# Attention's RMS of parts 4 and 5 taken with tokens on partitions

## What is computed

```python
out = (x - mean) * rsqrt(var + 1e-5) * weight + bias          # layer norm
x = (out + tanh(cond @ lin_w.T + lin_b)) * weight + bias
x = x + a_alpha * attention(a_gamma * rms(x) + a_beta)        # 16 heads of 16
x = x + f_alpha * (silu(h @ gate_w.T) * (h @ hidden_w.T) @ out_w.T + out_b),  h = f_gamma * rms(x) + f_beta
```

## Time and profile before

| | |
|---|---|
| median of 3 runs | 960.4 us (960.19 to 960.7) |
| the profiled execution's own time | 959.94 us |
| its span | 958.1 us |
| granted TensorE clock | 0.999 |
| busy: PE, DVE, ACT, POOL | 919.5, 740.5, 634.9, 501.0 us |

### The profile page before, as it was taken

One profiled execution on the slowest core, in us unless ns is written; L12 is line 12 of the kernel. 1 busy time (PEld: TensorE's weight loads), 2 busy tenths in 40 slices (PEclk: granted clock), 3 DMA queues, 4 the chain that ended last, 5 costly groups with the idle time before them and its releaser, 6 DMA issues.

```text
span 958.1 us, 28583 instructions
## 1 busy us (share of the span) xinstructions
PE 919.5 (96%) x11064; PEld 883.9 (92%) x11064; DVE 740.5 (77%) x1433; ACT 634.9 (66%) x1837; POOL 501.0 (52%) x479
## 2 busy tenths in 40 slices
PE   5667999999999999999999999999999999999997
PEld 4557999999999999999999999999999999998997
DVE  5977788788778778877877887887788787667654
ACT  3656766767776776777677677767667766766432
POOL 4686455465655555555455555545555555453320
PEclk9999999999999999999999999999999999999999
DMA  6200011120020212002121210202110110100000
GB/s 224 75 2 29 13 24 56 25 51 22 10 57 24 57 24 51 13 18 57 23 57 24 49 12 20 58 24 56 25 36 23 24 36 18 18 13 13 13 12 24
DMA packets 40631, 33.77 MB, mean 35 GB/s; under 512 B 10800, under 2 KB 39984, under 8 KB 40496
## 3 DMA queue, kind: packets, MB, share of 16 engines
q1 hardware_dynamic: 40496, 31.93, 13.3%
HBM read 23.37 MB, written 8.55 MB: 33 GB/s over the span
## 4 chain that ended last, share of the span: by engine, by line
PE 89%; DVE 5%; issue 3%; POOL 2%; ACT 1%; DMA 0%; SPq 0%; DVEq 0%; ACTq 0%; POOLq 0%
PE psum L361 18%; PE psum L363 18%; PE psum L362 18%; PE psum L587 6%; PE psum L589 6%; PE psum L588 6%; PE psum L521 5%; PE psum L495 4%; PE psum L537 4%; PE psum L396 2%; PE psum L415 1%; DVE least L743 1%; PE psum L408 1%; POOL probs L1270 0%; DVE row_sum L759 0%
## 5 line engine op out<-in xcount | busy, mean ns | idle before, releaser
L361 PE MATMUL psum<-xf_hi,ffn_hi 128*128 128x256 f32 x1024 | 291.3, 284 | 2.1 <-ACT probsT L1055 1.6
L362 PE MATMUL psum<-xf_lo,ffn_hi 128*128 128x256 f32 x1024 | 288.1, 281 | 0.0
L363 PE MATMUL psum<-xf_hi,ffn_lo 128*128 128x256 f32 x1024 | 287.8, 281 | 0.0
L1047 ACT ACTIVATE probs<-psum,least 128x64 f32<-128x64 f32 x928 | 204.5, 354 | 38.5 <-DVE least L743 37.7
L1270 POOL TENSOR_TENSOR probs<-probs,inv_sum 128x512 f32<-128x512 f32 x128 | 133.9, 1047 | 154.1 <-DVE inv_sum L764 154.0
L361 PEld LDWEIGHTS psum<-xf_hi,ffn_hi 128*128 128x128 f32 x1024 | 192.7, 188 | 3.2 <-issue 2.7
L362 PEld LDWEIGHTS psum<-xf_lo,ffn_hi 128*128 128x128 f32 x1024 | 192.8, 188 | 0.0
L363 PEld LDWEIGHTS psum<-xf_hi,ffn_lo 128*128 128x128 f32 x1024 | 192.8, 188 | 0.0
L1076 ACT ACTIVATE prod_hi<-late 128x512 fp32r<-128x512 f32 x128 | 83.3, 651 | 127.6 <-DVE late L827 127.5
L587 PE MATMUL psum<-prod_hi,ffn_hi 128*128 128x256 f32 x512 | 144.1, 281 | 0.9 <-DVE prod_lo L833 0.9
L589 PE MATMUL psum<-prod_hi,ffn_lo 128*128 128x256 f32 x512 | 144.1, 282 | 0.0
(11 more groups left out here) (116 smaller groups left out, 2154.4 us busy)
## 6 DMA issues: line engine op xcount, KB each, us to landing
out_t_dram<-x_res SPq DMA_DIRECT2D x31, 256.0 KB, 3.0
xin<-x_dram SPq DMA_DIRECT2D x15, 512.0 KB, 6.7
shift_tok<-shift_rows SPq DMA_DIRECT2D x104, 64.0 KB, 3.1
inv_row<-inv_rows SPq DMA_DIRECT2D x26, 128.0 KB, 4.8
w_raw<-attn_w_dram SPq DMA_DIRECT2D x1, 1024.0 KB, 6.7
x_res<-gate_w_dram SPq DMA_DIRECT2D x1, 1024.0 KB, 9.4
late<-hidden_w_dram SPq DMA_DIRECT2D x1, 1024.0 KB, 11.3
w_raw<-out_w_dram SPq DMA_DIRECT2D x1, 1024.0 KB, 6.4
```

The costliest lines, as they stand in the source:

```text
L361: pe.matmul(out, stat_hi, mov_hi, start=first, stop=False)
L362: pe.matmul(out, stat_hi, mov_lo, start=False, stop=False)
L363: return pe.matmul(out, stat_lo, mov_hi, start=False, stop=last)
L1047: op = act.activation(probs[g % 4][:, h * SEQ:(h + 1) * SEQ], scores[g % 2][:, h // 2, h % 2], ACT.Exp, bias=least[g % 2][:, h:h + 1], sca ...
```

## The change

`ROW_FROM` goes from 6 to 4, so that parts 4 and 5 (block 2) are handled in the second way. A new function `root_due(s)` names the part whose inverses are taken and sent in slot `s`: for parts 4 and 5 in the last slot (`j == 3`) of the group ahead, slots 7 and 11, and for the later parts in the first slot of their group, as before. VectorE's residual, ScalarE's squares and GpSimd's sums of these parts, and GpSimd's `normalise_tokens` of block 2, go. `attention_out(1)` no longer waits for `scaled_a`.

```diff
--- before.py
+++ after.py
@@ -64,7 +64,7 @@
 SPLIT_ORDER = [c for chunks in SPLITS.values() for c in chunks]
 OUT_W_AT = -3
 QUAD = 32
-ROW_FROM = 6
+ROW_FROM = 4
 
 
 def conditioned_block(nc, x, cond_t, mod_w, feat_vecs, attn_w, gate_w, hidden_w, out_w, identity, head_mask, out_t):
@@ -221,6 +221,10 @@
             if not ROW_FROM // 2 <= b < NBLK or k not in (0, 1, 2, 4):
                 return None
             return 4 * b + min(k, 3)
+
+        def root_due(s):
+            m = (s + 1) // PSEQ + 2 if s < FFN_AT else s // PSEQ + 2
+            return m if row_part(m) and s % PSEQ == (3 if s < FFN_AT else 0) and s != FFN_AT else None
 
         def tile_no(i):
             return i - 2 * ROW_FROM
@@ -337,8 +341,8 @@
                     sp.dma_start(shift_rows, rows[:, D:2 * D]).then_inc(table_sent, 16)
                 if tile_at(s + 1) is not None:
                     load_shift(tile_at(s + 1))
-                if s % PSEQ == 0 and row_part(s // PSEQ + 2):
-                    send_inverses(s // PSEQ + 2)
+                if root_due(s) is not None:
+                    send_inverses(root_due(s))
                 if (s + 4) % (2 * PSEQ) == 0 and (s + 4) // (2 * PSEQ) + 2 < NBLK:
                     b = (s + 4) // (2 * PSEQ) + 2
                     sp.wait_ge(x_turned, 2 * (b - 1))
@@ -463,7 +467,8 @@
             def attention_out(m):
                 pe.wait_ge(att_lo_made, m + 1)
                 if early_out(m):
-                    pe.wait_ge(scaled_a, m + 4)
+                    if turns_a(m + 1):
+                        pe.wait_ge(scaled_a, m + 4)
                     if m >= 1:
                         pe.wait_ge(scaled_f, m)
                 else:
@@ -892,13 +897,13 @@
                     mean_squares_out(grp)
                 if is_step(f - 1):
                     product_lo(f - 1)
-                if j == 0 and row_part(grp + 2):
-                    token_squares_out(grp + 2)
+                if root_due(s) is not None:
+                    token_squares_out(root_due(s))
                 if j == 1 and tile_at(s) is not None and tile_at(s) % TILES == 3:
                     shift_tokens(tile_at(s))
                 if s == 0:
                     scale_a(1)
-                if j == 0 and PSEQ <= s <= FFN_AT:
+                if j == 0 and PSEQ <= s <= FFN_AT and not row_part(grp + 2):
                     make_residual(grp + 2)
                 if s % 2 == 0:
                     for g in (s, s + 1):
@@ -1130,10 +1135,10 @@
                 if s == 0:
                     split_hi_a(1)
                 if wide(s) and j == 0 and s > 0:
-                    square_a(grp + 2)
+                    if turns_a(grp):
+                        square_a(grp + 2)
                     keys_out(grp + 1)
                 if s == FFN_AT:
-                    square_a(grp + 2)
                     keys_out(grp + 1)
                     square_f(grp - 2)
                 if s % 2 == 0 and is_seq(s):
@@ -1289,7 +1294,8 @@
                     apply_beta_a(1)
                     split_lo_a(1)
                 if j == 0 and 0 <= s < FFN_AT:
-                    sum_squares_a(grp + 2)
+                    if turns_a(grp):
+                        sum_squares_a(grp + 2)
                     if is_part(grp - 2):
                         sum_squares_f(grp - 2)
                 if j == 2 and 0 <= s < FFN_AT:
@@ -1304,10 +1310,8 @@
                     if s == FIRST_SLOT:
                         half_rstd(1)
                     apply_gamma_a(grp + 2)
-                if s == FFN_AT:
-                    sum_squares_a(grp + 2)
-                if j == 0 and row_part(grp + 2):
-                    token_inverse(grp + 2)
+                if root_due(s) is not None:
+                    token_inverse(root_due(s))
                 if j == 0 and is_part(grp - 2) and not wide(s):
                     sum_squares_f(grp - 2)
                     apply_gamma_f(grp - 2)
@@ -1333,10 +1337,6 @@
                     add_attention(grp - 1)
                 if j == (grp == 1) and grp % 2 == 1 and 1 <= (grp + 3) // 2 < NBLK:
                     token_rstd((grp + 3) // 2)
-                if grp == 1 and j == 1:
-                    normalise_tokens((grp + 3) // 2, 0)
-                if grp == 1 and j >= 1:
-                    normalise_tokens((grp + 3) // 2, j)
                 if j == 1 and 0 <= grp - 4 < NPART - 1:
                     add_ffn(grp - 4)
```

## The result

The changed kernel took 972.04 us (median of 4 runs, 970.22 to 973.45) where the kernel before took 960.31 (4 runs): ratio 1.012, 95% interval 1.0103 to 1.0138. It is slower, as forecast, but by 11.7 us instead of 7.1, and outside the range. On another chip it took 971.14 against 962.00, ratio 1.0094 (1.0073 to 1.0115). The profiled execution took 972.41, its span is 970.6 us.

The account below looks back on a forecast made before the run. Up to slot 12 a chain through VectorE, GpSimd, ScalarE and TensorE sets the pace, then a full TensorE. +8.2 − 1.05 = +7.15 us on 959.94 gives 967.1, forecast as a median of 967.5 us, range 963.0 to 970.5.

Parts of the forecast that it names:

- Step 1: Slot 5, VectorE: tile 8's shift waits for block 2's `rstd` from GpSimd, making `find_least(6)` 3.9 us later.
- Step 3: Slot 7, VectorE: `token_squares_out(4)` waits for tile 9's square, idling 2 us; `gate_attention(0)` 6.6 us later.
- VectorE's old slack: Slot 7: VectorE's idle 3.45 us before its weight split absorbs part, so `find_least(8)` is +3.7, not +6.6.
- Step 5: SP's queue: the send of part 4's inverses holds tile 11's shift rows, making `find_least(10)` 8.2 us later (+6.5 to +12.5).
- Step 6: Slots 10, 11: +8.2 reaches the FFN's start; second send holding tile 12's load costs nothing, or up to 1.8 us.
- Rivals A: No queue wait: SP's write returns under about 3 us or shift rows land by 74; 963.4 us, chance 0.14.
- B: Relief wins: GpSimd's and VectorE's saved work in slots 5 to 8, with step 7, gives 956.5 us; chance 0.05.
- C: Slack takes it: idle time of slots 7 and 11 swallows the waits, gains pay the rest; 960.4 us, chance 0.06.
- Rival D: More sends collide: second send also holds tile 12's shift rows, write slow both times; +11, 971 us, chance 0.05.
- Step 4: Slot 8: TensorE's transposes, products and scores take 1.8 us after `gate_attention(0)`; `find_least(8)` 3.7 us later.
- Step 7: From slot 12: 0.6 us won from ScalarE's own residual copy, 0.45 from part 5's dropped TensorE transposes; −1.05 us.

Follow-up runs that it names:

- the second profile of the change: The changed kernel run again, unedited, on another chip: 971.14 us against 962.00 for the kernel before.
- the first wait gone: Changed kernel with GpSimd's `token_rstd(2)` moved from the end of slot 5 to the start of slot 4: 968.72 us against 962.55.
- the two fillings that kept the clock up: Changed kernel with values of parts 2 and 3 computed three times, 971.19 us; all three waits moved, part 3's values and part 1's output product computed twice, 964.51 us.
- the waits gone: Changed kernel with `token_rstd(2)` in slot 4, tile 11's shift load ahead of the send, `token_squares_out` of parts 4 and 5 behind `gate_attention`: 964.85 us against 962.00.
- the pair of runs with the clock up and down in slot 12: Changed kernel with values of parts 2 and 3 computed three times, 971.19 us; with part 3's alone and tile 12's shift load ahead of the second send, 971.67 us.
- taking it away: Changed kernel with tile 11's shift load issued in slot 7, ahead of the send of part 4's inverses: 969.26 us against 962.55.
- the first filled one: Changed kernel with the values of parts 2 and 3 computed three times over: 971.19 us.
- the second filled one: Changed kernel with part 3's values computed three times and tile 12's shift load issued in slot 11 ahead of the second send: 971.67 us.
- the first way taken early: Kernel before, with GpSimd's `token_rstd(2)` and two `normalise_tokens` of block 2 taken in slot 4 instead of slot 5: 961.05 us against 962.00.
- the wait alone: Kernel before, with VectorE only made to wait for block 2's inverse deviation at the end of slot 5: 965.35 us against 962.55.
- with its gap filled: Kernel before with that VectorE wait at the end of slot 5, and part 2's values computed three times: 962.42 us against 962.00.

## Why the prediction was wrong

**Right.** Step 1 to a tenth: `find_least(6)` +3.9, released by GpSimd's power. Step 3: VectorE's `gate_attention(0)` +6.5 against +6.6, though with 0.8 us of idle time instead of 2, because the shift of tile 9 itself took longer (below). That VectorE's old slack would take part of it is right too. Step 5's mechanism is right: SP's send holds the shift rows of tile 11. Step 6's worry is right, and the profiles ran into it: tile 12 was held for 0.4 us in the second profile of the change, 0.6 with the first wait gone, and 1.8 and 1.7 in the two fillings that kept the clock up. Rivals A, B and C are out, and with the waits gone the change still loses 2.9 us. Rival D's 971 was close to both medians by luck: its slow writes took 8.1 and 8.3 us instead of 9.3, and tile 12 waited for 0 or 0.4 us.

**The step that failed: TensorE's durations in steps 4 and 6.** I took them from a trace in which the clock never fell. Step 4 put that trace's 1.8 us for the transposes, products and scores; step 6 had the +8.2 of `find_least(10)` arrive unchanged at the FFN's start. I had read TensorE's idle time before slot 7's output product as harmless, though my own step 1 opened it from 0.5 to 4.4 us. The sum needed:

- slot 8: `find_least(8)` +5.1 instead of +3.7. The group from the transposes of slot 8 to its scores took 67.24 to 70.43, 3.2 us for 1.8.
- slots 11 and 12: +9.2 at `find_least(10)`, and still +9.2 at the last transposes of `probs`, became +10.9 at the end of the scores. All of these 1.8 us are in the four groups at half clock.

That this is the clock's doing, and that it reaches slot 13, is shown by the pair of runs with the clock up and down in slot 12. That it would have reached the end was not shown by undoing it.

**Step 5 was mis-sized, in a way that hid the first of these.** I had VectorE reach tile 11's wait 2.7 us earlier than it did and so put the wait at 4.2 us; it was 1.9, and taking it away won 2.3 to 2.5. The wait covered what slot 8 lost, so the 1.4 us there never reached the end. The send's 8.07 us instead of 7.4 was inside the bounds, and the landing (about 4.0) was as taken. `find_least(10)` was +9.2 for a forecast of +8.2: 0.45 of that is the later landing, and 0.5 the shift itself, which took 0.97 us instead of 0.48. The ends that I gave for this step, +6.5 and +12.5, are +6.1 and +12.7 by the rows.

**Step 7.** Of 0.6 us in slot 13, about 0.46 was seen (TensorE's idle time of 1.98 is 1.52 now):

```profile
102.38 0.41 PE L412 MATMUL psum<-ident,square_sum_f 128*128 128x128 f32 x2 [1.52 <-issue]
```

The same 0.46 is there between the scores of slot 12 and slot 13 in the two fillings whose clock stayed up. Of the transposes' 0.45, 0.43 is there between slots 13 and 15, and a loss of 0.5 us later (0.4 in the second profile), which I haven't placed, cancels it.

Together the 3.5 us between +10.63 and the forecast's +7.15 are 1.0 from step 5, 1.8 from step 6 and 0.7 from step 7.

The rest of the miss against the range, 1.5 us above its upper end, is of the size of the early clock loss (1.87 us in this profile, 0.2 in the next); whether the other three timed runs had it is not known. With it taken out the change costs 10.3 to 10.6 us against the one profile of the kernel before, which is at the range's edge and still 3.1 to 3.5 over the forecast.

## What to carry over

A wait that an in-order engine takes on costs what stands behind it on the queue, and also what its consumer's idle time does to TensorE: after such a step, look at how long TensorE will now idle and what clock it had behind gaps of that length. When a blocking send is moved one slot forward, list the loads that it has jumped over. And before a chain is rebuilt, ask whether the work that made it slow can simply be issued earlier: here that gave 1 us where the new way lost 9.

## What was not expected of the hardware

TensorE's granted clock fell from 2.4 to 1.2 GHz around the output products of slots 7 and 11 in both profiles of the changed kernel, where the engine had been idle for 4.3 to 4.4 us, and the groups behind them still ran at half clock. Idle times of some 2 us ahead of the last transposes of `probs` in slot 11 went either way. The clock stayed full in the profile of the kernel before (79.77 us) and in the first filled one (88.88, after 1.87 us). It fell in the second filled one (89.31), in the first way taken early (78.06), and with the wait alone, without and with its gap filled (83.02 and 83.88). The last three have slot 11 as the kernel before has it, so some of its own executions may lose the clock there too: its mean clock ran from 0.990 to 1.000. Part of the losses that the experiments show in slots 12 and 13 may then be chance and not their edits.

VectorE's two-input instruction of 0.48 us (L712) took 1.38 at 64.21 and at 67.56 (and 0.97 at 80.37), while GpSimd ran two-input instructions on SBUF at its side, which stretched as well (1.46 us for 1.27, 1.36 for 1.28):

```profile
63.86 1.46 POOL L1248 TENSOR_TENSOR xn_lo<-normed_a,xn_hi 128x512 fp32r<-128x512 f32 x1
65.27 1.23 POOL L1275 TENSOR_TENSOR probs<-probs,inv_sum 128x512 f32<-128x512 f32 x1
```

In the steady part the same instruction took 0.483 to 0.487 us in all of its 52 instances, but the one ahead of it, the centring (L703 in the kernel before), up to 1.52 (minimum, median and maximum in ns):

```profile
L703 DVE SCALAR_TENSOR_TENSOR xin<-xin,mean,rows x52: 474/480/1518, 94.1 to 795.7; 128x256 f32<-128x256 f32 x52
```

The Trainium skill's page "GPSIMD Engine Reference", section "Specifications", says that GpSimd's SBUF interface is shared with VectorE and is contended by VectorE's instructions with two SBUF inputs. The rows at 63.86 and 65.27 agree with it; no run here separates the two engines. A price for an added VectorE instruction should be taken beside GpSimd's work, not from a quiet place.
